# A graph-network layer in pipelined steps: VectorE's gamma scaling between output and seed, the edge index behind the edge scaling, ScalarE's copy of merged rows behind n_gT and the seeds

## The reference, cut to what matters

```python
# x: 50000 x 128, edge_attr: 25000 x 128, src/dst: 25000, dst sorted; all float32
h = jnp.maximum(_layernorm(x, axis=-1), 0.0)
xn = layernorm(h, g1, b1)
msg = jax.nn.relu(xn[src] + edge_attr)
aggr = jax.ops.segment_sum(msg, dst, num_segments=N)
u = (1.0 + eps_gin) * xn + aggr
u = jax.nn.relu(u @ Wg1 + bg1) @ Wg2 + bg2
h2 = h + u
xn2 = layernorm(h2, g2, b2)
f = jax.nn.gelu(xn2 @ Wf1 + bf1, approximate=False) @ Wf2 + bf2   # Wf1: 128 x 512, Wf2: 512 x 128
return x + (h2 + f)
```

## Time and profile before

| what | value |
|---|---|
| median of three runs | 1058.03 us |
| the profiled execution's own time | 1055.18 us |
| its span, first to last instruction | 1053.4 us |
| TensorE / VectorE / ScalarE / GpSimd busy | 94% / 93% / 81% / 77% |
| granted TensorE clock, mean | 0.985 |
| DMA | 149 GB/s mean |

### The profile page before, as it was taken

One profiled execution on the slowest core, in us unless ns is written; L12 is line 12 of the kernel. 1 busy time (PEld: TensorE's weight loads), 2 busy tenths in 40 slices (PEclk: granted clock), 3 DMA queues, 4 the chain that ended last, 5 costly groups with the idle time before them and its releaser, 6 DMA issues. The chain is left out here.

```text
span 1053.4 us, 23086 instructions
## 1 busy us (share of the span) xinstructions
PE 987.0 (94%) x6684; PEld 848.8 (81%) x6684; DVE 975.7 (93%) x3499; ACT 855.4 (81%) x2158; POOL 814.8 (77%) x510
## 2 busy tenths in 40 slices
PE   1459999999999999999999999999999999999998
PEld 0347888888888888888888888888888888888877
DVE  5789999999999999999999999999999999998742
ACT  1258888988988888888888889889889888887863
POOL 6788888888888878888888888888888888875620
PEclk9779999999999999999999999999999999999999
DMA  8765766788785654554554555555555455443221
GB/s 267 203 174 129 215 171 174 230 237 236 241 246 153 154 135 114 144 143 116 138 138 126 136 142 126 125 147 131 119 149 135 112 154 130 103 120 86 58 61 40
DMA packets 110468, 156.87 MB, mean 149 GB/s; under 512 B 24835, under 2 KB 50607, under 8 KB 110334
## 3 DMA queue, kind: packets, MB, share of 16 engines
q1 hardware_dynamic: 70358, 128.99, 38.0%
q0 software_dynamic: 37760, 25.66, 17.7%
q10 hardware_dynamic: 2216, 0.66, 0.3%
HBM read 90.61 MB, written 64.61 MB: 147 GB/s over the span
## 5 line engine op out<-in xcount | busy, mean ns | idle before, releaser
L447 POOL DMA_INDIRECT aggr_sums<-e_merged,e_index x196 | 325.7, 1662 | 59.4 <-issue 51.6
L920 PE MATMUL p_out<-wf,n_act 128*128 128x128 f32 x3136 | 366.2, 275 | 0.0
L920 PEld LDWEIGHTS p_out<-wf,n_act 128*128 128x128 f32 x3136 | 358.0, 192 | 0.0
L456 POOL TENSOR_TENSOR n_rstd<-n_var,minus_half 128x16 f32<-128x16 f32 (+3 forms) x102 | 257.7, 2537 | 90.2 <-DVE n_var L819 36.8
L522 ACT ACTIVATE n_act<-p_f,bf1e_col 128x512 f32<-128x512 f32 x392 | 255.9, 679 | 31.1 <-PE p_f L883 26.1
L436 POOL DMA_INDIRECT e_x<-in_x,e_cols x196 | 226.4, 1155 | 60.2 <-issue 59.1
L883 PE MATMUL p_f<-n_z2T_high,wf_low 128*128 128x512 f32 x392 | 208.6, 532 | 11.1 <-ACT n_act L522 8.5
L883 PE MATMUL p_f<-n_z2T_high,wf_high 128*128 128x512 f32 x392 | 155.2, 396 | 0.0
L883 PE MATMUL p_f<-n_z2T_low,wf_high 128*128 128x512 f32 x392 | 154.6, 394 | 0.0
L604 ACT ACTIVATE n_inT<-p_in 128x512 f32<-128x512 f32 x98 | 58.5, 596 | 109.6 <-PE p_in L927 106.9
L675 DVE BATCH_NORM_STATS2 n_stat<-n_x 128x6 f32<-128x256 f32 x392 | 139.9, 418 | 0.1
(11 more groups left out here) (85 smaller groups left out, 1463.5 us busy)
## 6 DMA issues: line engine op xcount, KB each, us to landing
n_x<-in_x SPq DMA_DIRECT2D x97, 256.0 KB
n_aggr<-aggr_sums SPq DMA_DIRECT2D x97, 256.0 KB, 2.7
out_dram<-n_out SPq DMA_DIRECT2D x97, 256.0 KB
aggr_sums<-zeros SPq DMA_DIRECT2D x26, 512.0 KB, 5.2
e_dst<-in_dst_rows SPq DMA_DIRECT2D x49, 256.0 KB
e_attr<-in_attr SPq DMA_DIRECT2D x48, 256.0 KB
aggr_sums<-zeros SPq DMA_DIRECT2D x12, 1024.0 KB
e_x<-in_x,e_cols POOLq DMA_INDIRECT x196
```

The lines of the kernel that those rows point to most:

```text
L447: nc.gpsimd.indirect_dma_start(out=aggr, out_offset=bass.IndirectOffsetOnAxis(ap=e_index[0:r, s, j:j + 1], axis=0), in_=e_merged[0:r, s, j ...
L456: return nc.gpsimd.tensor_tensor(n_rstd[0:r, s, lo:hi], n_var[0:r, s, lo:hi], minus_half[0:r, 0:(hi - lo) * J].rearrange("p (a j) -> p a j ...
L920: last = nc.tensor.matmul(p_out[0:b.rows, j, :], n_act[:, k, j, 0:b.rows], wf2[:, k, :], start=False, stop=(k == KF - 1), skip_group_check ...
```

## The change

Three orders are changed, no instruction is added or removed.

```diff
@@ ScalarE, step @@
                     seed_gout(b, (0, 1))
-                if 1 in halves and 0 not in halves:
-                    merged_rows(edge(3))
                 if (b := node(6)) is not None:
                     gelu(b, 1)
                 if (b := node(3)) is not None:
                     hidden(b)
                     seed_gout(b, (2, 3))
+                if 1 in halves and 0 not in halves:
+                    merged_rows(edge(3))
@@ VectorE, second_half @@
-                    if not (c.fixed and c.k < 3):
-                        dve.wait_ge(q_scatter[s], SCATTERED * c.uses(3))
-                    dve.wait_ge(s_eextra, c.at + 1)
-                    nc.vector.tensor_tensor(e_index[0:r, s], e_dstf[0:r, s], e_extra[0:r, s],
-                                            ALU.max).then_inc(s_eindex, 1)
...
                     for j in range(J):
                         last = nc.vector.scalar_tensor_tensor(e_zg[0:r, s, j, :], ...)
                     last.then_inc(s_ezg, 1)
+                    if not (c.fixed and c.k < 3):
+                        dve.wait_ge(q_scatter[s], SCATTERED * c.uses(3))
+                    dve.wait_ge(s_eextra, c.at + 1)
+                    nc.vector.tensor_tensor(e_index[0:r, s], e_dstf[0:r, s], e_extra[0:r, s],
+                                            ALU.max).then_inc(s_eindex, 1)
@@ VectorE, step @@
-                if (b := node(6)) is not None:      # seed of p_out: s_x2, s_nout, s_x2b
...
                 if (b := node(1)) is not None:      # four n_zg, as before
...
                     last.then_inc(s_nzg, 1)
+                if (b := node(6)) is not None:
+                    r = b.rows
+                    dve.wait_ge(s_x2, b.at + 1)
+                    reached(dve, s_nout, b.at)
+                    nc.vector.tensor_tensor(p_out[0:r], n_x2[0:r, b.slot(4)], n_x[0:r, b.slot(8)],
+                                            ALU.add).then_inc(s_x2b, 1)
```

More of the change, by code:

```diff
@@ L827, in step @@
                                             ALU.add).then_inc(s_nout, 1)
-                if (b := node(6)) is not None:
[L829 to L833, removed]
                 if (b := node(1)) is not None:
```

## The result

| | median us | own time of the profiled execution | span |
|---|---|---|---|
| before | 1058.05 (four runs) | 1055.18 | 1053.4 |
| changed | 1048.36 (1047.66 to 1049.93, four runs) | 1047.92 | 1046.2 |

The ratio is 0.9915, with a 95% interval of 0.9901 to 0.9929: faster by 9.7 us. Forecast were 18.0. The time lies inside the wide range of 1034 to 1053, but outside the forecast's own 1035 to 1045. A later set of runs of the same kernel, on another chip, gave 1046.09 and 0.9890 (0.9871 to 0.9909).

What follows compares the result with a forecast made beforehand. VectorE was taken to set the pace at 19.91 us per pair, falling to 19.42: 40.7 x 0.49 = 19.9, less 0.5 for the sums and 1.4 at the end, gives 1058.03 - 18.0 = 1040.0 us (1035 to 1045; wide range 1034 to 1053).

Steps and rivals of the forecast that it cites:

- What bounds: VectorE sets the pace from about 100 to about 913 us, 19.91 us per pair of steps; TensorE alone needs 19.31.
- parts 1 and 2: VectorE: the seed behind `n_zg` saves 0.19 us per step, 0.38 per pair; `e_index` behind `e_zg` saves 0.11 per pair.
- The rival that VectorE saves nothing: Gaps of 0.79 and 0.18 are VectorE's own spacing; only the end's +1.4 us remains: about 1059 us, chance 0.09.
- Part 3: ScalarE's later copy: TensorE's second-half step shrinks from 9.49 towards 9.00 us; the copy, 1.72 later, stays hidden in steady part.
- Part 4: At `p_out` of the first-half step TensorE waits 0.3 us for the later seed, a one-time shift, not per pair.
- ring: Late seed delays TensorE, ScalarE's `n_z2T_high`, VectorE's `z2_low` and the next seed in turn: about 1076 us, slower, chance 0.07.
- Part 5: At `n_in` of second-half steps loaded sums have 0.8 us to spare, about 0.4 after the change; 0.5 allowed in all.
- The forecast's own sign of being wrong: Wrong if the gap moves to `n_zg`, the pair is 19.6 us or more, or VectorE waits for `n_z2T_high` or the sums.
- second limit close behind: TensorE or the loads of the sums bind just behind VectorE, losing half of the 0.49 us: about 1049, chance 0.18.
- Part 6: Kernel's end: the last chunk's first scatter pays the copy's 1.72 us in full; with nearby steps' gains and losses, net +1.4.
- The sum: 40.7 pairs x 0.49 = 19.9 us, less 0.5 and 1.4: 18.0 us saved, from 1058.03 to 1040.0.

Runs made afterwards that it cites:

- the seed back: The changed kernel with the seed of `p_out` back between `n_out` and `n_zg`: 1055.29 us, one run.
- the index back: The changed kernel with `e_index` back ahead of `e_zg`: 1054.66 us, one run.
- ScalarE's part only: The kernel before with only ScalarE's copy of the merged rows moved later, VectorE as before: 1060.10 us, ratio 1.0025.
- last copy early: The changed kernel with only the last chunk's copy of the merged rows put back ahead of GELU 1: 1045.78 us, ratio 0.9878.

## Why the prediction was right in direction and wrong in size

**What bounds, and parts 1 and 2: right.** The seed was worth 0.18 and 0.20 in the two steps, `e_index` 0.12 (0.19 and 0.11 forecast), the undisturbed pair 19.39 (19.42). The rival that VectorE saves nothing is refuted by the seed back and the index back: the gap stands with the dependent instruction and goes with it. The Trainium skill (VectorE: DVE Perf Modes, "The DRAIN you can't avoid") says of eight `tensor_copy` in a row that the semaphore costs nothing extra. That doesn't carry over to these instructions: 0.79 with the wait against 0.60 without, 0.19 against 0.08 for 128x4.

**Part 3: right, but for one wait.** TensorE's wait for ScalarE at k = 3 stood in all 39 second-half steps between 110 and 900 us before (23.5 us) and in none of the 40 of the changed kernel. TensorE's step became 8.99, and without the copy's move VectorE's saving was worth 2.7 us. That the copy is hidden in the steady part is right for the time, since moving it back to the front changed no mean pair. It isn't hidden for the scatter, which starts 0.5 us later. In the medians over the steps of the traces it starts 0.20 after the end of GpSimd's power or 0.87 to 0.88 after the end of the copy, whichever comes last. The copy ends 4.20 after `n_x2` in ScalarE's part only, where 4.20 + 0.88 is just the 5.08 of before, and 4.75 in the changed kernel, where the scatter starts at 5.62. I had set the copy's end (506.0) against the scatter's start (506.85) and left out the 0.87.

**Part 4: nearly right.** (The seed's lateness by the rows is 4.51 - 4.28 = 0.23, where I wrote 0.3.) TensorE waits for the seed at `p_out` 21 times, 5.4 us; the waits shrink to 6 times and 1.9 us once the sums are taken later, so most of them look like the sums' disturbance seen from TensorE. No ring closed: VectorE has no listed wait for `n_z2T_high` in the changed kernel.

**Part 5, the loaded sums: the step that failed.** I put "0.8 to spare", "About 0.4 is left" and "I allow 0.5 us in all". The 0.38 that VectorE sheds was right; the spare, the DMA side and the spread were not. The forecast's own sign of being wrong came: a mean pair of 19.6 or more, with VectorE waiting for the sums.

- The spare was 0.54, not 0.8. I took a median landing by adding 2.7 to one issue, and `n_in` as able to start on it. Where `n_in` waits it starts 0.19 after the last landing: 4.60 - 3.87 - 0.19 = 0.54.
- VectorE took 0.39 of it: 0.19 by the shorter first-half step and 0.20 by `n_in` itself. That would have left 0.15. The scatter and the load, which I had taken as unchanged, took another 0.39: 0.06 by a later start of the scatter, 0.18 by its length, 0.09 from its end to the issue, 0.06 in the load. 0.54 - 0.39 - 0.39 = -0.24: the mean chunk is late.
- Then the spread counts. From the scatter's end to the load's issue it is 1.62 to 2.47 us before, which the spare hid, and 1.64 to 3.38 in the changed kernel. Why the longest grew is open.

The price: 19.70 - 19.39 = 0.31 per pair, 0.31 x 38 = 11.8 us, of which 11.0 stand directly ahead of `n_in`, against 0.5 allowed. (The kernel before has 0.04 x 38 = 1.5 of such losses in three pairs, nearly all of it elsewhere; the balance of the two kernels is 10.3.) That is the rival "second limit close behind" (about 1049), with the loads as the limit. I had counted against it that each slack "is still positive by the rows"; the rows were single ones.

**Part 6, the end: too small.** TensorE's block 84 starts 10.25 us earlier (919.94 to 909.69), the span is 7.2 shorter, so 3.0 are lost after it, against 1.4. The copy's 1.73 was forecast at 1.72. Beyond it, the last full block's `n_in` starts 0.80 later after the last chunk's third scatter (13.24 before, 14.04 changed), and from there to the end it takes 1.18 longer (43.65 and 44.83), nearly all of it at a lower clock (see the last section). Against these stands a gain of 0.72 between blocks 84 and 90: 1.73 + 0.80 + 1.18 - 0.72 = 3.0. The 13.24 is 13.24 to 13.52 in the seven kernels with the last copy early and 13.39 to 14.04 in the eight with it late, so part of the 0.80 seems to go with the copy; why isn't shown.

**The sum.** On the profile's scale: 19.0 won in 38 pairs and some 1.5 in those before and after them, 10.3 given back, nearly all at `n_in`, 3.0 at the end: 7.2. The medians differ by more, 9.7 and, in the second set, 11.0; single executions of the changed kernel vary by 2 us, and the profiled one of before was 2.9 under its median.

## What to carry to other kernels

When a change makes the pace-setting engine faster, take for each thing that it waits for the distribution of landing times over all steps, not one row and a median, and compare it with where the engine will then stand; a slack of half a microsecond with a spread as large is already a cost. A gap ahead of an instruction that depends on its predecessor on the same engine is real time that an independent instruction can fill. Two changes may each be worth little or less than nothing alone (here 2.7 and -2.3 us) and much together (9.7); and once an engine waits for a load, a place later in its own queue for the consumer can be the cheap remedy: here it gave 5 to 8 us, while a shorter scatter ahead of the load gave none.

## What the runs showed of the hardware that I had not expected

**A scatter's length by VectorE's neighbour.** GpSimd's indirect scatter takes 1.58 us when it starts ahead of VectorE's first `e_match`, 1.80 to 1.91 when 0.05 to 0.20 us into it, 1.59 when 0.4 to 0.75 behind its start, and an `e_attrb` under its end makes no difference. The Trainium skill (SBUF — State Buffer, "Who interferes with whom") says that a VectorE instruction with two SBUF inputs contends with a GpSimd instruction that reads SBUF. `e_match` has two SBUF inputs, so the 1.80 to 1.91 may be such a case, but the traces don't bear the rule out as it stands: a scatter that starts ahead of the four `e_match` runs beside all of them in 1.58, one that starts 0.4 to 0.75 behind starts inside the second or third of them and takes 1.59, and `e_attrb`, also with two SBUF inputs, did nothing at the scatter's end. What is held, and when, stays open.

**The clock after a wait.** Near the end TensorE waits for the last sums. Its rows, changed:

```profile
1002.54 1.11 PE L927 MATMUL p_in<-ident,n_in 128*128 128x128 f32 x4 [5.35 <-DVE n_in L848]
1003.30 0.78 PE L883 MATMUL p_f<-n_z2T_high,wf_low 128*128 128x512 f32 x1
```

Before:

```profile
1010.98 0.66 PE L927 MATMUL p_in<-ident,n_in 128*128 128x128 f32 x4 [2.33 <-DVE n_in L848]
1011.57 0.50 PE L883 MATMUL p_f<-n_z2T_high,wf_low 128*128 128x512 f32 x1
```

The granted clock by the view of windows was 0.72 from 1000 to 1006 us of the changed kernel (0.50 from 1002.5 to 1004.5) and 1.00 from 1009 to 1015 before, so TensorE spent part of the first at 1.2 GHz and all of the second at 2.4; the same product takes 0.78 us and 0.50. It looks as if the longer wait (5.35 us against 2.33) had brought the lower clock. The other traces don't bear this out. With the last copy early the same wait is 2.50 us and the clock fell all the same, while TensorE was already at work again (0.72 from 1000 to 1006, 0.50 from 1002 to 1004):

```profile
1000.34 0.66 PE L929 MATMUL p_in<-ident,n_in 128*128 128x128 f32 x4 [2.50 <-DVE n_in L850]
1000.94 0.68 PE L885 MATMUL p_f<-n_z2T_high,wf_low 128*128 128x512 f32 x1
```

All eight traces with a wait of 4.67 to 5.35 us here have the lower clock behind it; of the seven with 1.97 to 2.62 us four have it (2.09, 2.11, 2.50, 2.62) and three don't (1.97, 2.33, 2.51). So the lower clock can follow a wait of that size and needn't; what decides isn't settled by these traces. The price is plain: from the `n_in` that ends the wait to the end of the kernel it takes 43.6 to 43.7 us in the three traces at full clock and 44.7 to 46.1 in the others. That is also why the theory of the last copy early, which put the lower clock down to the longer wait, was not borne out.
